# A gated cross-attention kernel: a square, a score and a store change their places

## The reference

```python
memory_proj = einsum('bme,de->bmd', memory, W_mem)
scores = einsum('bnd,bmd->bnm', x, memory_proj) / sqrt(D)
attn = softmax(scores, axis=-1)
memory_context = einsum('bnm,bmd->bnd', attn, memory_proj)
gate = sigmoid(einsum('bnf,df->bnd', concatenate([x, memory_context], -1), W_gate) + b_gate)
fused = x + gate * memory_context
out = fused * rsqrt(mean(fused**2, -1) + EPS) * norm_w
```

## Time and profile before

| | before |
|---|---|
| device time, median of 3 runs | 306.37 us (305.67 to 306.54) |
| span of the profiled execution | 304.1 us |
| granted TensorE clock, mean | 0.990 |
| TensorE busy | 291.3 us, 96% |
| VectorE busy | 189.7 us, 62% |
| ScalarE busy | 172.2 us, 57% |
| GpSimd busy | 171.1 us, 56% |
| transfers | 50.24 MB, 165 GB/s |

### The profile page before, as it was taken

How to read it: one execution, slowest core, us unless ns; L and a number is a source line. 1 busy time by engine, 2 the same in 40 slices (tenths; PEclk the granted TensorE clock), 3 DMA queues, 4 the chain that set the end, 5 groups by cost and what they waited for, 6 DMA issues and landing times.

```text
span 304.1 us, 5140 instructions
## 1 busy us (share of the span) xinstructions
PE 291.3 (96%) x1646; PEld 252.2 (83%) x1646; DVE 189.7 (62%) x321; ACT 172.2 (57%) x363; POOL 171.1 (56%) x137
## 2 busy tenths in 40 slices
PE   6978999999999999999999999999999999999992
PEld 3776988888889988878889998888889998888881
DVE  3695347787676237777667335788756326767755
ACT  5746555657736555656644645655754755555442
POOL 0174445785962745585981943585891753555402
PEclk9997999999999999999999999999999999999998
DMA  7976651757663352756744353584745253443001
GB/s 215 388 264 207 196 166 59 245 175 229 200 195 117 107 181 88 244 185 164 264 149 143 119 173 102 143 284 110 252 160 183 70 171 102 138 150 128 34 37 69
DMA packets 24941, 50.24 MB, mean 165 GB/s; under 512 B 2272, under 2 KB 8672, under 8 KB 24928
## 3 DMA queue, kind: packets, MB, share of 16 engines
q1 hardware_dynamic: 24928, 50.08, 50.9%
HBM read 42.73 MB, written 7.34 MB: 165 GB/s over the span
## 4 chain that ended last, share of the span: by engine, by line
PE 85%; DVE 6%; ACT 3%; DMA 2%; issue 1%; SPq 1%; DVEq 0%; POOL 0%; POOLq 0%; ACTq 0%
PE gate_ps L278 35%; PE ctx_ps L278 13%; PE am_bank L278 12%; PE q_ps L278 11%; PE score_ps L278 11%; PE pT_ps L318 3%; DVE work L647 2%; DMA work<-in_wgT 2%; PE am_bank L335 2%; DVE wgx_lo L601 2%; ACT work L497 1%; ACT wgc_hi L465 1%; DVE top L613 1%; DVE xT_lo L601 1%; DVE pT_lo L601 1%
## 5 line engine op out<-in xcount | busy, mean ns | idle before, releaser
L758 POOL TENSOR_TENSOR memT_lo<-memT_raw,memT_hi 128x752 fp32r<-128x752 f32 x32 | 59.5, 1859 | 74.2 <-ACT memT_hi L465 74.2
L758 POOL TENSOR_TENSOR mem_lo<-mem_raw,mem_hi 128x768 fp32r<-128x768 f32 x32 | 59.1, 1846 | 3.5 <-ACT mem_hi L465 3.5
L278 PE MATMUL gate_ps<-wgx_hi,xT_hi 128*128 128x512 f32 x112 | 44.8, 400 | 0.0
L278 PE MATMUL gate_ps<-wgx_hi,xT_lo 128*128 128x512 f32 x112 | 44.4, 397 | 0.0
L278 PE MATMUL gate_ps<-wgx_lo,xT_hi 128*128 128x512 f32 x112 | 44.2, 395 | 0.0
L573 ACT ACTIVATE am<-am_bank,share 112x256 f32<-112x256 f32 x32 | 15.3, 477 | 49.4 <-PE am_bank L278 49.4
L647 DVE SCALAR_TENSOR_TENSOR work<-work,x_rows 128x512 f32<-128x512 f32 (+1 forms) x29 | 40.9, 1415 | 0.7
L601 DVE TENSOR_TENSOR pT_lo<-pT_ps,pT_hi 128x336 fp32r<-128x336 f32 x32 | 16.2, 507 | 36.4 <-ACT pT_hi L465 36.4
L655 DVE SCALAR_TENSOR_TENSOR work<-work,rstd,norm_w 128x512 f32<-128x512 f32 (+1 forms) x29 | 35.1, 1213 | 1.0 <-POOL rstd L819 1.0
L490 ACT ACTIVATE probs<-score_ps,shift 112x375 f32<-112x375 f32 x32 | 18.4, 575 | 28.5 <-DVE shift L615 28.5
L758 POOL TENSOR_TENSOR xT_lo<-xT_raw,xT_hi 128x1280 fp32r<-128x1280 f32 (+1 forms) x10 | 32.4, 3241 | 0.0
(11 more groups left out here) (99 smaller groups left out, 744.0 us busy)
## 6 DMA issues: line engine op xcount, KB each, us to landing
mem_raw<-in_mem SPq DMA_DIRECT2D x32, 384.0 KB, 4.0
memT_raw<-in_memT SPq DMA_DIRECT2D x32, 376.0 KB, 3.1
x_rows<-in_x SPq DMA_DIRECT2D x28, 256.0 KB, 4.2
out<-work SPq DMA_DIRECT2D x27, 256.0 KB, 4.4
xT_raw<-in_xT SPq DMA_DIRECT2D x8, 640.0 KB, 6.7
xT_raw<-in_xT SPq DMA_DIRECT2D x3, 512.0 KB, 5.0
work<-in_wgT SPq DMA_DIRECT2D x2, 512.0 KB, 6.9
x_rows<-in_wgT SPq DMA_DIRECT2D x2, 512.0 KB, 9.9
```

What stands on the lines that cost most here:

```text
L278: mm = pe.matmul(out, left, right, start=first and i == 0, stop=last and i == n - 1)
L758: return pool.tensor_tensor(out, in_, high.bitcast(F32), ALU.subtract)
```

## The change

Three edits, each of them a change of order or of queue; no arithmetic changes.

1. ScalarE's `square` of tile `b - 3` now comes behind the copy `pT_hi` in each batch from 3 on, in all groups.
2. At the end of groups 0 to 2, TensorE does q01 ahead of `context` of tile 6 and the next group's first score ahead of q10. VectorE does `q_low` of q01 ahead of `gate_context` of tile 6 and the maximum ahead of `fuse` of tile 6. ScalarE does the exponentials ahead of `square` of tile 6.
3. The second half of the last output tile is stored from ScalarE's queue, not from SyncE's.

```diff
@@ block.sync, the end
-            for i, cols in enumerate(HALVES):
-                sp.wait_ge(y_ready, TILES * GROUPS + i)
-                sp.dma_start(out_d[TILES * GROUPS - 1][:, cols], y[:, LAST_SLOT, cols]).then_inc(y_stored[LAST_SLOT], 16)
+            cols = HALVES[0]
+            sp.wait_ge(y_ready, TILES * GROUPS)
+            sp.dma_start(out_d[TILES * GROUPS - 1][:, cols], y[:, LAST_SLOT, cols]).then_inc(y_stored[LAST_SLOT], 16)
@@ block.tensor, the end of a group
                     q_piece(g + 1, 0, 0)
                     gate_am(g, TILES - 1)
+                    q_piece(g + 1, 0, 1)
                     context(g, TILES - 1)
-                    q_piece(g + 1, 0, 1)
+                    score(g + 1, 0)
                     q_piece(g + 1, 1, 0)
-                    score(g + 1, 0)
@@ block.scalar, a batch
-                    if b >= 3:
-                        square(g, b - 3)
                     if b in (1, 2):
                         q_high(g, 2, b - 1)
                     act.wait_ge(pT_done, GROUP * g + b + 1)
                     high(pT_hi[:, b % 2], probsT).then_inc(pT_hi_ready, 1)
+                    if b >= 3:
+                        square(g, b - 3)
@@ block.scalar, the end of a group and of the program
                     q_high(g + 1, 0, 0)
                     tanh(g, TILES - 1)
                     q_high(g + 1, 0, 1)
+                    exponentials(g + 1, 0)
                     square(g, TILES - 1)
                     q_high(g + 1, 1, 0)
-                    exponentials(g + 1, 0)
...
             group(GROUPS - 1, True)
+            cols = HALVES[1]
+            act.wait_ge(y_ready, TILES * GROUPS + 1)
+            act.dma_start(out_d[TILES * GROUPS - 1][:, cols], y[:, LAST_SLOT, cols]).then_inc(y_stored[LAST_SLOT], 16)
@@ block.vector, the end of a group
                     q_low(g + 1, 0, 0)
                     add_bias(g, TILES - 1)
                     norm(g, TILES - 2)
+                    q_low(g + 1, 0, 1)
                     gate_context(g, TILES - 1)
-                    q_low(g + 1, 0, 1)
+                    maximum(g + 1, 0)
                     fuse(g, TILES - 1)
-                    maximum(g + 1, 0)
                     q_low(g + 1, 1, 0)
                     norm(g, TILES - 1)
```

## The result

The changed kernel takes **311.48 us** (median of 4 runs, 311.32 to 311.99) against 306.02 us for the kernel before in the same series (305.51 to 306.54): a ratio of 1.018, 95% interval 1.014 to 1.021. It is 5.5 us slower where 4.3 were forecast. The profiled execution took 311.99 us with a span of 310.2 us, so 1.8 us lie around the span; before, the span was 304.1.

The account below looks back on a forecast made before the run. TensorE's own stream, 96% busy, was taken as the bound. 3 x (1.85 - 0.42) = +4.3 us on a 304.1 us span gives 308.4, plus 2.3 around it: 310.7 us; own range 309.9 to 311.5, overall 307.8 to 312.4.

Parts of the forecast that it names:

- The hole at batch 5 closes, 0.42 each: TensorE's wait for `pT_lo` in batch 5 of groups 0 to 2 goes: -1.26 us for three groups.
- GpSimd's backlog of 0.88: The later square delays GpSimd's last `xT_lo` of a group, and VectorE's fuse of tile 5, by 0.88 us.
- the normalisation held behind `mem_lo`: VectorE's normalisation L655 stands behind GpSimd, moving maximum and exponentials by at most 0.88 us, covered by 1.2 us.
- Rival A: GpSimd's 0.88 shift is absorbed, leaving TensorE 0.97 us idle before the first score: 308.0 us; chance 0.10.
- The order at the group's end, 0.92 to 1.07: Reordering makes the next group's first score ready 0.92 to 1.07 us after TensorE wants it.
- The sum of the hole, 1.85: TensorE's new wait before the next group's first score, reordering plus GpSimd delay: 1.85 us, three times, +5.55 us.
- The last hop: From VectorE's `qT_lo` start to TensorE's first score at the group's end: 0.47 us.
- The store, 0: Storing the last half tile from ScalarE's queue changes nothing; bounds are a 0.41 us gain or about as much loss.
- Rival B: TensorE's clock falls in each of three new group-end waits: +3.1 to +6.9 us, 313.8 to 317.6; chance 0.07.
- My two witnesses: Clock evidence before: a fall after TensorE's 3.1 us wait at the start, none after 0.42 us waits at batch 5.
- Rivals C: VectorE's fuse of tile 5 isn't held by `xT_lo`; new wait 0.2 us at most: 305.1 to 305.7; chance 0.06.
- D: TensorE's batch 5 wait stays because shares and `pT_lo` stand behind VectorE's fuse: 312.0 us; chance 0.05.

Follow-up runs that it names:

- the earlier `q_low`: Kernel before with the square behind `pT_hi` from batch 3 on, and VectorE's `q_low` of q01 ahead of `gate_context`: 305.19 us, ratio 0.998.
- the run with batch 5 alone: Kernel before with ScalarE's square behind the copy `pT_hi` in batch 5 only, in all groups: 304.2 us, ratio 0.994.
- the version that the runs point to: Kernel before with the square behind `pT_hi` in batch 5 only and the start's one GpSimd `xT_lo` cut into four: 301.66 us, ratio 0.987.
- with quarters at the start: Changed kernel with only the start's GpSimd `xT_lo` issued as four instructions: 308.41 us, ratio 1.009 to the kernel before.
- the order alone: Kernel before with only the reordering at the group's end on TensorE, VectorE and ScalarE: 309.25 us, ratio 1.013.
- the square in 3 to 5: Changed kernel with the square behind `pT_hi` only in batches 3 to 5, ahead again in 6 and 7: 307.67 us, ratio 1.006 to the kernel before.
- the quarters: Changed kernel with each GpSimd split `xT_lo` issued as four instructions: 305.43 us, ratio 0.999 to the kernel before.
- the filler: Changed kernel with eight zero products on TensorE before the next group's first score: 311.34 us; again, 310.00 against 311.61 unfilled.

## Why the prediction was right, point by point

*The hole at batch 5 closes, 0.42 each.* Right, and a little more than priced: the step from batch 5 to 6 went from 8.61 to 8.11 us, 0.50. A hole costs its length and up to 0.1 for the first matmuls behind it. In the changed kernel there is luck in it: the prediction took the fuse of batch 5 to be held still, to 65.04, but GpSimd's delay reached batch 5 too and let the fuse go first (62.98 + 1.35 = 64.33). That the square's place alone closes the hole is shown by the run with batch 5 alone, where the fuse is held for 2.31 us.

*GpSimd's backlog of 0.88.* Right, and so is the normalisation held behind `mem_lo`, which no wait of TensorE shows, so it was covered. The backlog is 0.87 in the profile, and worth 0.84 of each hole when it alone was taken away (1.95 against 1.11). Rival A, that it is absorbed, is refuted. The slack that I took to be missing in batches 6 and 7 exists in batch 5, which is why the square there can move for nothing.

*The order at the group's end, 0.92 to 1.07.* Right in kind, 1.10 alone.

*The sum of the hole, 1.85.* The term that was mis-sized: 1.95, with 2.05 paid, by which the forecast's difference would have been 3 x (2.05 - 0.50) = 4.65 and not 4.3. The chain from the fuse's end to the start of `qT_lo` was worked out as 3.04 (88.73 to 91.77) and took 3.05 (89.27 to 92.32). The last hop was off: 0.47 from `qT_lo` to TensorE, taken over from `pT_lo`; it is 0.66 (92.32 to 92.98, and 93.65 to 94.31 with the square alone). The same 0.19 is what the expectations for the square alone (0.60 for 0.44) and for the earlier `q_low` (0.27 for 0.1) missed. TensorE's longer idle time isn't the reason. In the version that the runs point to, TensorE idles 0.95 us ahead of an attend at the start (the last gate matmul starts at 24.46), and attend begins 0.54 after the start of `pT_lo`:

```profile
25.10 0.48 DVE L603 TENSOR_TENSOR pT_lo<-pT_ps,pT_hi 128x336 fp32r<-128x336 f32 x1
...
25.64 0.38 PE L278 MATMUL am_bank<-mem_hi,pT_hi 128*112 128x256 f32 x1 [0.79 <-DVE pT_lo L603]
```

Why the hop to the score is longer stays open.

*The store, 0.* Right: ratio 1.001 with an interval that reaches 1.000.

*Rival B, the clock falls in the hole.* I gave it 0.07 and set it apart from the forecast; it was part of the outcome. Of nine holes of some 2 us in three profiled executions (the changed kernel twice, and with quarters at the start), four were followed by a fall, each worth 1.5 to 1.6 us (18.15 against 16.56). That is inside the price of 1.0 to 2.3 that the rival had for one hole; what it had wrong is that all three would fall. None followed the nine holes of 1.1 to 1.3 us in the profiles of the order alone, of the square in 3 to 5, and of the quarters, nor the six holes with the filler, and between the start and the last matmuls no profile of any run shows a fall in another place. My two witnesses, a hole of 3.1 with a fall and holes of 0.42 without, left the question open just where the new hole was; a chance of a half for a part of the cost would have been nearer.

For the profiled pair this accounts for the distance: 4.65 us, and one fall of 1.6, are some 6.2; the span grew 6.1. The medians grew 5.5, and of their distance from 4.3 the holes' size explains 0.35; that falls make up the rest is argued, since no profile was taken of the other executions. The mean granted clock doesn't settle it, for it doesn't tell where the clock fell: the kernel before has means of 0.985 to 0.999 too, and its profile shows a fall at the start alone. So at a group's end, by the profiles, a fall came only behind an unfilled hole of about 2 us, and not behind each; that products of zeros prevent it is likely (no fall behind six filled holes, 1.6 us between the medians on one chip) but not shown. The first run of the filler, with clocks of 0.983 to 0.990, doesn't bear it out; whether the clock fell there at the start or in other places stays open.

*Rivals C and D* didn't come: the fuse of tile 5 was held until 0.55 after `xT_lo`, and batch 5 had no hole. For D the run with batch 5 alone is the test, since in the changed kernel the fuse was early.

*The total.* The forecast of 310.7 came within 0.8 us of 311.48, partly by luck. It added 2.3 us around the span, from a median and a span of different executions; in the profiled execution after it is 1.8. The wrong 0.5 made up for a part of what was missing. Its own range, redone from its terms, is 310.1 to 311.7 and not 309.9 to 311.5; 311.48 lies in both. A single run needn't: one on another chip took 313.96.

## What to carry to other kernels

Before an instruction is moved back on one engine, follow what it releases to the next engine's queue: here a square moved by 0.9 us delayed two tiny GpSimd instructions, behind them subtractions of up to 3.4 us that hold VectorE, and the bill came two batches later at a loop's end. Move it only where that queue has idle time. And when work is put ahead of a consumer to get it done early, check that its operands are ready by then; a long instruction on an engine that can hold another one is worth cutting into pieces where it stands on the way.

## What the runs showed that I had not expected

Cutting one GpSimd instruction of 3.4 us at the start into four made the whole kernel some 2 us faster (3.8 with the square of batch 5, which alone gives 1.8) and the changed one 3.2, though the four take 4.3. VectorE got its turn in between, and in the three profiles with these quarters the clock stayed up at the start. A hole in TensorE's stream costs up to 0.1 us more than its length (0.50 for 0.42, 0.66 for 0.60, 1.19 for 1.10, 2.05 for 1.95). And equal kernels differ from run to run, the changed one by 4.6 us in six runs (309.33 to 313.96), the one before by 3.6 in eleven on the same chip (304.07 to 307.68). In the profiles the clock falls behind some holes and not behind others, at the start in both kernels and at the group ends in the changed one.
